# A two-layer graph network on one core: adjacency packed 512 rows at a time from casting loads, and the epilogue of layer 0 on VectorE

## The reference

```python
# layer 0: attention over the neighbours
Wh = h @ W
e = (Wh @ a1)[:, None] + (Wh @ a2)[None, :]
e = where(e > 0, e, 0.2 * e)
e = where(adj > 0, e, -9e15)
h_prime = softmax(e, axis=1) @ Wh
x = layernorm(x + elu(h_prime))
# layer 1: mean over the neighbours
deg = sum(adj, axis=1)
x = layernorm(x + concat([adj @ x / deg, x]) @ weight + bias)
```

## Time and profile before

| what | us |
|---|---|
| median of three runs (1591.59 to 1591.82) | 1591.62 |
| the profiled execution | 1587.96 |
| its span | 1586.1 |
| PE busy in the span | 1544.6 (97%) |
| DVE busy | 871.8 (55%) |
| ACT busy | 999.9 (63%) |
| POOL busy | 437.1 (28%) |
| layer 0's products on PE begin | 54.70 |
| layer 1's products on PE begin | 1073.22 |

### The profile page before, as it was taken

The page is one execution under the profiler, slowest core; times in us unless marked ns, Lnnn a source line. Parts: engine busy times, 40 slices in busy tenths (PEclk is TensorE's granted clock), DMA queues, the critical chain, the costliest instruction groups (busy, mean ns, idle before and its releaser), DMA issues. The chain is left out here.

```text
span 1586.1 us, 46438 instructions
## 1 busy us (share of the span) xinstructions
PE 1544.6 (97%) x16966; PEld 1369.4 (86%) x16966; DVE 871.8 (55%) x3335; ACT 999.9 (63%) x2513; POOL 437.1 (28%) x571
## 2 busy tenths in 40 slices
PE   7599999999999999999999999999999999999998
PEld 6488888888888888888888888887888888888886
DVE  7965655565556555555555555564454544444443
ACT  3999899989998999899989998971000101000000
POOL 0033443344334433443354335430000000000000
PEclk9799999999999999999999999999999999999999
DMA  8567877877777787777777887742000000000000
GB/s 276 228 266 276 292 278 284 278 284 278 285 283 279 278 287 276 285 279 287 283 278 278 285 287 279 280 133 55 17 17 17 18 19 17 17 17 17 17 17 17
DMA packets 100732, 302.84 MB, mean 191 GB/s; under 512 B 5728, under 2 KB 67936, under 8 KB 67936
## 3 DMA queue, kind: packets, MB, share of 16 engines
q1 hardware_dynamic: 100704, 302.48, 53.7%
HBM read 289.77 MB, written 12.68 MB: 191 GB/s over the span
## 5 line engine op out<-in xcount | busy, mean ns | idle before, releaser
L476 ACT ACTIVATE level_ring<-s_row,cols 128x256 fp8e4<-128x256 f32 x2048 | 839.8, 500 | 0.0
L688 PE MATMUL acc<-factors,edge_ring 128*128 128x258 f16 x4096 | 581.8, 272 | 11.0 <-DVE edge_ring L933 6.6
L688 PE MATMUL acc<-factors,level_ring 128*128 128x258 f16 x4096 | 581.4, 272 | 0.0
L646 PE MATMUL pack_ps<-pack_w,adj_ring 128*128 128x8 bf16 x4096 | 544.8, 170 | 11.9 <-DMA adj_ring<-in_adj 11.9
L753 PE MATMUL acc<-factors,adj_ring 128*128 128x258 f16 x4096 | 468.3, 273 | 3.5 <-DMA factors<-x_parts 2.0
L753 PEld LDWEIGHTS acc<-factors,adj_ring 128*128 128x128 fp8e4 x4096 | 399.0, 97 | 61.6 <-DMA factors<-x_parts 2.3
L688 PEld LDWEIGHTS acc<-factors,edge_ring 128*128 128x128 fp8e4 x4096 | 387.6, 97 | 66.0 <-issue 11.9
L688 PEld LDWEIGHTS acc<-factors,level_ring 128*128 128x128 fp8e4 x4096 | 396.4, 97 | 55.7
L646 PEld LDWEIGHTS pack_ps<-pack_w,adj_ring 128*128 128x128 fp8e4 x4096 | 387.8, 97 | 14.1 <-DMA adj_ring<-in_adj 12.2
L926 DVE TENSOR_TENSOR level_ring<-level_ring,edge_ring 128x1024 uint16<-128x1024 uint16 x256 | 177.0, 693 | 236.9 <-ACT level_ring L476 226.0
L584 ACT ACTIVATE part_sums<-acc 128x258 f32<-128x258 f32 x32 | 12.4, 387 | 294.2 <-PE acc L753 294.2
(11 more groups left out here) (101 smaller groups left out, 838.8 us busy)
## 6 DMA issues: line engine op xcount, KB each, us to landing
adj_ring<-in_adj SPq DMA_DIRECT2D x128, 2048.0 KB, 7.7
x_parts<-parts SPq DMA_DIRECT2D x32, 129.0 KB, 3.1
factors<-x_parts SPq DMA_DIRECT2D x8, 516.0 KB, 4.0
factors<-in_x SPq DMA_DIRECT2D x8, 512.0 KB, 7.2
s_row<-s_and_t SPq DMA_DIRECT2D x32, 128.0 KB, 4.9
rows_x<-in_x SPq DMA_DIRECT2D x32, 128.0 KB, 3.1
x_rows<-rows_y SPq DMA_DIRECT2D x32, 128.0 KB, 7.5
rows_x<-x_rows SPq DMA_DIRECT2D x32, 128.0 KB, 2.1
```

The costliest lines, as they stand in the source:

```text
L476: a = act.activation(level_bytes[:, h % MASK_SLOTS, j, :, :], s_halves[:, slot, :, :], ACT.Relu, bias=t_big[:, h * HALF + j:h * HALF + j + ...
L646: return pe.matmul(words_t, low_bytes, pack_w[:, :], start=True, stop=True)
L688: m = pe.matmul(acc[a][:, 0:ROW], mask, factors[:, neg, jj, :], start=(jj == 0), stop=(jj == NJ - 1))
```

## The change

It has five parts.

1. **Loads.** `adj` comes 512 rows at a time (row block `n` of 16; two groups `q` = 0, 1 share it). `load_adj` moves from SP's queue to POOL's, reads int32 and writes uint8: 4 MB read and 1 MB written for each of the four chunks, into four slots, one for each chunk. On POOL's queue the loads stand between the `inverse_deviation` steps.
2. **Joining.** DVE joins the bytes of four row tiles into one byte whose low four bits are four rows: a shift-and-or of 1024 int32 elements and, waiting for it, one of 512.
3. **Packing.** 16 packing products a chunk with 32 columns each, 64 for two groups' rows in place of 256; they follow every second product of the halves h = 3 and h = 7. `unpack` takes 4 instructions of 512 words for each chunk and group.
4. **Epilogue of layer 0.** POOL's part goes to DVE, as does ACT's `normalise`; POOL keeps the two small steps of `inverse_deviation`. On DVE `normalise(g-2)` stands after the masks of chunk 0, `add_low_sums`, `find_empty`, `fill_empty`, `invert_sum` and `divide` of g-1 between the steps of chunk 2, `low_parts(g-2)` after it, and `elu_and_residual(g-1)` with the statistics at the end of the group. On ACT `high_parts(g-2)` stands after h = 1 and `exponential(g-1)` after h = 6. On SP's queue `load_s` goes ahead of `store_x1`.
5. **Layout.** The two tiles of a group lie one behind the other in the masks' bytes, no longer alternating.

```diff
-ADJ_SLOTS = 2
+ADJ_SLOTS = 4
...
-        adj_tiles = adj.rearrange("(g p t) c -> g p t c", g=NG, t=TPG)
+        adj_tiles = adj.rearrange("(n t p) c -> n p t c", n=NR, t=TILES)
...
         @block.gpsimd
         def _(pool):
+            def load_adj(n, c, first=False):
+
+                if not first:
+                    pool.wait_ge(packed, UPG * (n - 1) + c + 1)
+                    pool.sem_inc(adj_free, 1)
+                pool.dma_start(adj_ring[:, c, :, :], adj_tiles[n, :, :, c * COLS:(c + 1) * COLS]).then_inc(adj_in[c], 16)
...
+            loads(1, range(UPG))
+            inverse_deviation(TPG, mv_ok, var_ok, rstd_ok)
+            loads(2, range(UPG))
+            with pool.Fori(1, NR - 2) as n:
+                inverse_deviation(TPG * PAIR * n, mv_ok, var_ok, rstd_ok)
+                loads(n + 2, (0, 1))
+                inverse_deviation(TPG * (PAIR * n + 1), mv_ok, var_ok, rstd_ok)
+                loads(n + 2, (2, 3))
...
+            def group(g, slot, loads, next_words, before_last=None, second=False):
...
+                    if h == 1 and not second:
+                        high_parts(g - 2, before_last)
                     if h == 2:
                         copy_positive(g - 1, second)
-                    if h == 4:
+                    if h % 2 and h // 2 in next_words:
+                        copy_words(*next_words[h // 2])
+                    if h == 6:
                         exponential(g - 1)
...
+            with pe.Fori(1, NR - 1) as n:
+                group(PAIR * n, n + 1, {1: 0, 3: 1})
+                group(PAIR * n + 1, n + 1, {1: 2, 3: 3})
...
+            def join(n, c):
+
+                dve.wait_ge(adj_in[c], 16 * (n + 1))
+                pair = joined[:, c, :, :].rearrange("p (k t) c -> p t k c", t=TPG)
+                dve.scalar_tensor_tensor(out=pair[:, 0], in0=pair[:, 1], scalar=1, in1=pair[:, 0],
+                                         op0=ALU.logical_shift_left, op1=ALU.bitwise_or).then_inc(joined_tiles, 1)
+                dve.wait_ge(joined_tiles, UPG * n + c + 1)
+                dve.scalar_tensor_tensor(out=joined[:, c, 0, :], in0=joined[:, c, TPG, :], scalar=TPG,
+                                         in1=joined[:, c, 0, :], op0=ALU.logical_shift_left, op1=ALU.bitwise_or)\
+                    .then_inc(joined_ok, 1)
...
+            def masks(n, q, c, output=None, first=False):
+                g = PAIR * n + q
                 dve.wait_ge(mask_used, 8 * g + 2 * c + 2)
+                dve.wait_ge(words_ok, UPG * n + c + 1)
                 if output == "sums":
+                    add_negative(g - 1, first)
+                unpack(n, q, c, edge_ring, c % EDGE_SLOTS).then_inc(unpacked, 1)
+                if output == "softmax":
+                    add_low_sums(g - 1)
+                negative(g, c, 0)
+                if output == "softmax":
                     find_empty(g - 1)
+                negative(g, c, 1)
+                if output == "softmax":
+                    fill_empty(g - 1)
+                positive(g, c, 0)
+                if output == "softmax":
                     invert_sum(g - 1)
                 positive(g, c, 1)
+                if output == "softmax":
+                    divide(g - 1)
...
+            def group(n, q, joins, second=False, third=False):
+
+                g = PAIR * n + q
+                masks(n, q, 0)
+                if not second:
+                    normalise(g - 2, rstd_ok, x1_ok)
+                for c in joins.get(0, ()):
+                    join(n + 1, c)
+                masks(n, q, 1, "sums", second)
+                for c in joins.get(1, ()):
+                    join(n + 1, c)
+                masks(n, q, 2, "softmax")
+                if not second:
+                    low_parts(g - 2)
+                for c in joins.get(2, ()):
+                    join(n + 1, c)
+                masks(n, q, 3)
+                for c in joins.get(3, ()):
+                    join(n + 1, c)
+                elu_and_residual(g - 1, second)
...
+            group(0, 1, {c: (c,) for c in range(UPG)}, second=True)
+            with dve.Fori(1, NR - 1) as n:
+                group(n, 0, {0: (0,), 3: (1,)})
+                group(n, 1, {0: (2,), 3: (3,)})
+            group(NR - 1, 0, {})
+            group(NR - 1, 1, {})
```

More of the change, by code:

```diff
@@ L146, in adj_resnorm_kernel @@
         x_in_sem = [sem(f"x_in{k}") for k in range(NX // 2)]
-        adj_in = [sem("adj_in0"), sem("adj_in1")]
+        adj_in = [sem(f"adj_in{c}") for c in range(ADJ_SLOTS)]
         s_row_in = [sem("s_row_in0"), sem("s_row_in1")]
@@ L267, in _, with group @@
             sp.sem_inc(wh_saved, 1)
[L269 to L273, removed]
+            def group(g, slot, first=False, s_next=True):
+                if s_next:
+                    sp.wait_ge(score_ok, 8 * (g + 1))
+                    load_s(g + 2, slot)
                 if not first:
@@ L414, in output_0, with loads @@
-            def output_0(g, first=False):
-                softmax_rows(g)
-                elu_and_residual(g, first)
-                scale_and_shift(g)
-                low_parts(g)
-            pool.wait_ge(one_row_ok, 1)
-            output_0(0, first=True)
-            with pool.Fori(1, NG - 1) as g:
-                output_0(g)
-            scale_and_shift(NG - 1)
+            def loads(n, cs):
+                for c in cs:
+                    load_adj(n, c)
+            loads(1, range(UPG))
@@ L500, in high_parts @@
                 act.activation(parts[:, :, 0:F], rows_y[:, :, :], ACT.Copy, scale=X_SCALE).then_inc(high_part, 1)
-            def next_words(g, c, last=False):
-                if not (last and c >= 2):
-                    copy_words(g + c // 2, (c + 2) % UPG)
-            def normalise(g, first=False):
-                act.wait_ge(shift_ok, TPG * (g + 1))
-                if not first:
-                    act.wait_ge(low_part, g)
-                for b in range(TPG):
-                    act.activation(rows_y[:, b, :], rows_y[:, b, :], ACT.Identity, bias=shift[:, b:b + 1],
-                                   scale=rstd[:, b:b + 1]).then_inc(x1_ok, 1)
-            def group(g, slot, loads, second=False, last=False):
+            def group(g, slot, loads, next_words, before_last=None, second=False):
                 act.wait_ge(s_row_in[slot], 16 * loads)
@@ L997, in _ @@
                     make_product(2 * c + 3)
-                masks(0, c)
+                    join(0, c + 1)
+                masks(0, 0, c)
             dve.wait_ge(mean_made, 1)
@@ L1076, in _ @@
-            for c in range(UPG):
-                masks_1(0, c)
-            finish_layer_0()
+            for c in range(UPG):
+                masks_1(0, 0, c)
+            add_negative(NG - 1)
+            add_low_sums(NG - 1)
+            find_empty(NG - 1)
+            fill_empty(NG - 1)
+            invert_sum(NG - 1)
+            divide(NG - 1)
+            elu_and_residual(NG - 1)
+            normalise(NG - 1, rstd_ok, x1_ok)
+            low_parts(NG - 1)
             def wide_tile(i):
```

339 lines of the change are left out of this document (141 added, 198 removed).

## The result

The changed kernel took 1609.66 us (median of 4 runs, 1606.92 to 1610.53), the kernel before 1591.72 beside it (1591.59 to 1592.51): a ratio of 1.011 (1.009 to 1.013), **slower by 1.1%, 18 us**. The prediction said 1580, with a chance of 0.25 for slower; the range held the time. The profiled execution of after took 1609.33 us, with a span of 1607.4 for 1586.1 before.

A forecast was written before the change was run, and what follows sets the result against it. PE bound the old kernel at 31.6 us a group; ACT's and DVE's cycles of 31.0 would give 31.1. 28 groups saved 14.0; with start and end terms the sum was -11.3, hence 1580 us, range 1560 to 1640.

The forecast's parts named there:

- PE: Layer 0, each group: products plus 32 packing products need 28.6 + 0.7 = 29.4 us, 2.2 less than before.
- ACT: Layer 0, each group: 27.9 us of work, waits of 2.7 ahead of high_parts and 0.4 ahead of exponential, 31.0 in all.
- DVE's path: Layer 0, from h = 7's scores through join, elu and masks to high_parts: 9.55 us, plus ACT's 21.4, a 31.0 cycle.
- The second rival: DVE's path half a microsecond longer, by a 2.4 us join or POOL's descriptors: 31.6 a group, 1594 us; chance 0.15.
- The first rival: PE keeps the pace, ACT so far ahead that its high_parts wait costs nothing: 29.4 a group, 1531 us; chance 0.07.
- The prologue: Ahead of group 1 DVE sets the pace; PE ends group 0 at 101.0, ACT begins group 2 at 117.8: +1.3 us.
- once: +3.7: Row block 2's loads, queued behind group 0's statistics, bring DVE to 148.5 where ACT would ask at 144.8: +3.7 us.
- load_x has 6 us against 2.7 fixed: On SP's queue load_x goes out behind low_parts, with 6 us until elu_and_residual against a fixed 2.7.
- Loads: Layer 0's adj loads: 8.39 MB a group needs 270 GB/s, 410 taken; 13 us for 4 MB, landing some 15 us ahead.
- The third rival: Casting loads become the bound at join's wait on DVE: 1652 us at 250 GB/s, 1867 at 205; chance 0.18.
- Group 31: Last group of layer 0: ACT 29.9, DVE 1.5, two halves on PE 7.2, 38.6 us for 40.3 before: -1.7.
- The way into layer 1: Between the layers: normalise on DVE -1.0 us, add_negative behind group 30's end and four unpackings +1.5.

The follow-up runs named there:

- the join off the path: Changed kernel with the second join of groups 2 to 29 behind chunk 2's masks instead of chunk 3's: 1592.56 us.
- the fourfold packing: Changed kernel with every packing product issued four times, 128 a group as before the change: 1612.09 us.
- The run that mends groups 2 and 3 alone: Changed kernel with deviation steps done once early on an unused column, and row block 2's loads two ahead of group 0's deviations, two behind: 1598.47 us.
- the three warm-ups: Deviation steps run once early on an unused column, loads split two and two: high_parts behind h = 3 1536.38 and 1535.08 us, changed kernel 1598.47.

## Why the prediction was wrong

- **PE** (29.4 us a group): right, 29.38. Two products and one packing product of 32 columns read 0.248 us in PE's timeline, less 0.224 for the two: 0.025 for the packing product. The 29.7 of the other bound is excluded. The Trainium skill (TensorE: Matmul & The Clock Gate, Back-to-back issue gap) has a floor of about 25 ns, and the trace agrees.
- **ACT** (27.9 + 2.7 + 0.4 = 31.0): right. With the join off the path ACT's loop reads 30.96, of it 2.63 and 0.28 waits, so 28.05 of work.
- **DVE's path** (9.55 + 21.4 = 31.0): right as a mechanism, too short. In the row above, from the end of h = 7's scores (640.69, 0.20 ahead of the AND) to high_parts (651.17) it took 10.48, in the other groups 9.94 (609.39 to 619.33). The mean, 10.21, with 21.36 is 31.57. Missing were the 0.20 between two dependent elu steps, 0.13 ahead of the AND and 0.54 at the loop's head, half the time. The rows of before had shown no loop head of DVE's, and I did not look for one. This is the step that failed for the pace: 31.57 for 31.1, which on 28 groups are 13 us.
- **The second rival** gave this pace, 31.6, a chance of 0.15 and 1594 us. It named the wrong cause (a join of 2.4 us; it took 1.86), but the steady part of it is what came. The first rival's 29.4 was as right, and one line away: what spoke against it was true of the place of high_parts, not of the kernel.
- **The prologue** (PE ends group 0 at 101.0, ACT begins group 2 at 117.8): the measured 104.8 is 3.8 late and 123.53 is 5.7. DVE's products for the factors start 1.3 later than before (38.41 for 37.09), and DVE waits 2.05 for ACT's scores at 96.21, which no term had.
- **The step that failed at the start** is "once: +3.7", measured 13.3 (75.5 us from group 2's begin to group 4's, less 2 x 31.1), with "load_x has 6 us against 2.7 fixed". The loads were issued at 130.2 and landed at 144.2, 14.0 us later, near the 13 worked out. But DVE's wait for them held add_negative too, and so PE, for 8.04 us, and PE's packing behind it: ACT lost 4.41 and 4.11 us where 3.7 in all was taken. Then the burst of four casting loads that had gathered held load_x(1), 128 KB, for 15.3 us where the sum had 2.7, and with it DVE for 8.61 and ACT for 7.07. ACT began group 2 5.7 us later than forecast, group 3 11.1 (163.69 for 152.6), group 4 15.4 (199.07 for 183.7). The run that mends groups 2 and 3 alone gives back 11.2.
- **Loads**: right. No steady group waits for adj, and the load issued at 174.85, as the queue ran empty, landed 13.0 us later, as worked out, with DVE busy for its first 4 us. The third rival's mechanism, a lower rate of casting loads, fell. The 0.25 for slower and the upper end of the range rested mostly on it, so that the range held the time is luck.
- **Group 31** (38.6 us, by ACT's scores): measured 41.7. PE sets it: it begins the group behind ACT's copy_positive, at 1063.92, 13.1 us after ACT does, and then needs 256 x 0.112 = 28.6 us without a stop.
- **The way into layer 1** (+0.5): measured +2.5. PE's waits there grew by 1.0 us, and the lower clock behind the longer one cost some 1.6 more, a term that the sum did not have.

Sum against the forecast, to the end of layer 0: +15.4 at the start, +12.4 for 26 groups, +0.2 in group 30, +3.1 in group 31. The way into layer 1 adds 2.0, the rest of layer 1 gives back 0.5: 32.6 us between the -11.3 forecast and the +21.3 measured between the spans. The two steps named above as failed, the pace (+12.4) and the start's term (+9.6), are two thirds of it; either alone would have left the kernel within 2 us of before, together with the rest they make it slower. Nearly all of the loss against before is the start; PE's saving bought nothing, as the fourfold packing shows (+2.4 us).

## What to carry to other kernels

When work moves to another engine, look for the instruction that now waits for something made from what its own engine has just written: that wait recurs however far ahead the engine is, and it can eat a saving that is real. Where two loops are within a few per cent, price both from their own rows, idle gaps and loop heads included, and take one wait of each away by moving one line before the whole change is judged. At a pipeline's start, follow small transfers too, since a late burst of large ones holds them.

## What was not expected of the hardware

- Casting loads keep the rate: at full DMA share 105 GB/s of bytes are written, which is 420 GB/s read, for 410 of plain loads. Row of after, in the columns of the earlier trace rows:

```profile
145.00:147.00 2.00, 0.29 (x2) 0.26 (x3) 1.97 (x5) 2.00 (x7) 0.00 (x0) 0.50 1.04 105
```

  The Trainium skill (SBUF — State Buffer, SBUF: two separate sides) warns that DVE's two-port work keeps GpSimd from writing the descriptors of loads that it issues. No such loss is seen here, with DVE busy through the stretch; but all four loads had been issued by 137.8, and the trace does not show whether descriptors were still being written, so this is no test of it.
- A 128 KB load of rows_x on SP's queue took 15.3 us behind such loads, and the one before it 15.6, for a median of 3.0. Row of after, the loads of rows_x:

```profile
DMA to landing us min/median/max: 2.6/3.0/15.6
```

  The Trainium skill (DMA: Bandwidth & Descriptors, Queues, rings and completion order) has an engine take turns between queues packet by packet, by which a small load should pass a large one; here it came five times as late.
- GpSimd's first arithmetic step behind the all-reduces stood idle 7.6 to 9.9 us after it and its operands were ready, in the four runs that put two to four loads ahead of it without a warm-up (counted from mv where that came last), and 10.5 to 11.0 in the three warm-ups, whose second step also took 2.5 us for a usual 0.76. In the kernels where it had long stood idle ahead of mv nothing showed. The Trainium skill (GPSIMD Engine Reference, Instruction dispatch) gives the first call of newly loaded code some 6 us; here the idle time was longer, each time with casting loads in flight. Whether those lengthened it stays open.
- PE's waits of 2.3 us in the steady groups had two outcomes. Behind five of the nine that the trace shows between 300 and 900 us the granted clock was 0.50 to 0.58 for some 3 us, the lower of its two levels (1.2 of 2.4 GHz), and eight products took 1.93 us for 1.05. Behind the other four it stayed at 1.00, as it did behind waits of 1.76. So the length of the wait alone does not decide it; what does stays open. Rows of PE:

```profile
592.14 1.82 PE L617 MATMUL acc<-factors,edge_ring 128*128 128x258 f16 x8 [2.33 <-ACT part_sums L435]
593.75 1.93 PE L617 MATMUL acc<-factors,level_ring 128*128 128x258 f16 x8
...
655.29 1.05 PE L617 MATMUL acc<-factors,edge_ring 128*128 128x258 f16 x8 [2.32 <-ACT part_sums L435]
```
